# All high and low weights of a two-layer graph network moved to 32 modulo 128 bytes in each partition

## The chip, the cores and the metric

The kernel runs on one core of one Trainium2 chip. The metric is the device time in microseconds from start to end of one execution. A run of the kernel is an execution of one program; the median of three is compared.

## The reference

There are 50000 nodes with 256 features and 25000 edges with 64 features, sorted by target node. Everything is float32.

```python
h = relu(layernorm(x))                            # [50000, 256]
agg = segment_sum(edge_attr_64, dst, 50000)       # [50000, 64]
agg = agg / max(counts, 1)
hidden = relu(concat([agg, h], axis=1) @ W1 + b1) # W1 [320, 512]
out = x + hidden @ W2 + b2                        # W2 [512, 256]
```

## The kernel before

The nodes are cut into 98 tiles of 512 (`TILES`, `TILE`; the last has 336), and a tile into four groups of 128 (`SUB`). A tile goes through these stages, of which several tiles are under way at once, with X, HN, HQ, O and most other buffers in two copies:

- SyncE (SP) loads the node rows (`load_x`, L304) and for each group a window of edges (`load_windows`, L322 and L323), turns the normalised rows in quadrants (`move`), and stores the output (`store`).
- VectorE (DVE) takes the statistics and ScalarE (ACT) writes the normalised rows; DVE transposes them, and both split them into a high part that float32r holds exactly and a low rest (`HT_hi`, `HT_lo`). The means of the edge features come from a matmul with a one-hot matrix (`edge_means`, L893 to L898, reading `E_both` and `OH`) and lie in `QA` and `QB`.
- Layer 1 (`layer1_nodes`, L909 to L911, and `layer1_means`, L918 and L919) fills four PSUM banks, one for each 128 hidden units: high times high, high times low and low times high. In the matmuls of this layer the weights are the stationary operand, loaded by a weight load (PEld in the profile), and the activations are the moving operand of 512 columns.
- ACT writes the high half of the hidden layer (`H1_hi`, L611), DVE the low half (`H1_lo`, L729).
- Layer 2 (`layer2`) has the operands the other way round: the hidden layer is stationary, the weights `w2_both` move. L932 streams the high and the low weights of 128 hidden units in one go, 512 columns, against `H1_hi`; L934 streams the high ones alone, 256 columns, against `H1_lo`. DVE adds the halves and the residual (L740, L743).

The steps of layers 1 and 2 stand in `step`, whose order on TensorE (PE) is written out by hand: two groups of layer 1, the edge means of the next tile, two groups of layer 1, layer 2. Semaphores tie the engines together; each engine runs its own program in order.

The weights are read from memory once, in the start-up, into `w1_raw`, `wa_raw`, `ab_raw` and `w2_raw`. ACT copies them into the high tensors (`w1_hi`, `wa_hi`, `ab_hi`, and `w2_both[:, :, 0, :]` at L633), and GpSimd (POOL) subtracts these to get the low ones (`w1_lo`, `wb_lo`, and `w2_both[:, :, 1, :]` at L543). From then on TensorE alone reads them.

Every tensor in on-chip memory (SBUF) is a declaration `sb(name, shape)`, with the number of partitions first. The tensors lie one behind the other in each partition in the order of the declarations, each at the next multiple of 32 bytes. `ident`, the first, starts at a multiple of 128. The declarations up to the weights are these:

```python
        ident = sb("ident", [P, P])
        iota_row = sb("iota_row", [P, P])
        part_id = sb("part_id", [P, 1])
        base = sb("base", [P, TILES, SUB])
        half = sb("half", [P, SUB])
        eps = sb("eps", [P, SUB])
        ones_bf = sb("ones_bf", [P, 1], BF16)
        ones_f = sb("ones_f", [P, 1])
        b2_row = sb("b2_row", [P, D])
        w1_raw = sb("w1_raw", [P, CD, H])
        wa_raw = sb("wa_raw", [P, H])
        ab_raw = sb("ab_raw", [P, H])
        w2_raw = sb("w2_raw", [P, CH, D])
```

Here P is 128, D 256, H 512, CD 2, CH 4.

Of the kernel before, what the change touches and what calls it, by code (L numbers as in the profile page):

```python
# [14 lines left out]
P = 128  # L15
# [11 lines left out]
def build(nc, x, src, dst, edge_attr, w1, b1, w2, b2, out):  # L27
# [41 lines left out]
    with ExitStack() as ctx:  # L69
        def sb(name, shape, dt=F32):  # L70
            return ctx.enter_context(nc.sbuf_tensor(name, shape, dt))
# [18 lines left out]
        wa_raw = sb("wa_raw", [P, H])  # L90
        ab_raw = sb("ab_raw", [P, H])
        w2_raw = sb("w2_raw", [P, CH, D])
        w1_hi = sb("w1_hi", [P, CD, H], F32R)
        w1_lo = sb("w1_lo", [P, CD, H], F32R)
        wa_hi = sb("wa_hi", [P, H], F32R)
        wb_lo = sb("wb_lo", [P, H], F32R)
        ab_hi = sb("ab_hi", [P, H], F32R)
        w2_both = sb("w2_both", [P, CH, 2, D], F32R)


        dst_w = sb("dst_w", [EP, WIDE], I32)
# [920 lines left out]
```

## Time and profile before

| | us |
|---|---|
| median of 3 runs | 1345.34 (1344.73 to 1345.53) |
| the profiled execution, its own time | 1346.03 |
| its span, first to last instruction | 1344.4 |
| granted clock of TensorE over the span | 0.998 |

The profiled execution is one more run, 0.7 us above the median. Its span is 1.6 us less than its time, which is what lies around the instructions. In the page of the profile, busy time is a union of instruction durations per engine; a TensorE matmul's duration contains the tail of its pipeline, so that two neighbours overlap, and the distance between starts is what one costs. PE stands for the matmuls, PEld for the weight loads, which run beside the matmul ahead of them.

### The profile page before, as it was taken

What the parts mean: (1) busy time and instruction counts of PE and PEld (TensorE: products, weight loads), DVE (VectorE), ACT (ScalarE), POOL (GpSimd) and SP (SyncE); (2) the same over time, 40 slices, a digit from 0 to 9 for tenths busy, and PEclk for the clock granted to TensorE, in tenths of its full rate; (3) what the DMA queues carried; (4) which work ended last, traced back from release to release, by engine and by line L of the source; (5) the groups of instructions that cost most, each with busy time, mean ns of one, the idle gap of its engine ahead of it and who ended that gap; (6) DMA issues with size and microseconds to landing.
All of it is one profiled execution on the core that took longest, in us unless ns stands there. A gap on an engine that the chain in (4) does not pass through costs nothing.

```text
span 1344.4 us, 29244 instructions
## 1 busy us (share of the span) xinstructions
PE 1326.3 (99%) x6976; PEld 1118.6 (83%) x6976; DVE 1216.8 (91%) x3153; ACT 696.2 (52%) x1285; POOL 541.7 (40%) x707
## 2 busy tenths in 40 slices
PE   6999999999999999999999999999999999999998
PEld 3788888888888888888888888888888888888887
DVE  6899999999999999999999999999999999999997
ACT  5455555555555555555555555555555555555553
POOL 6443434343434343434343434343434343434341
PEclk9999999999999999999999999999999999999999
DMA  4676767676767676767676767676767666767663
GB/s 118 123 121 133 121 133 121 134 120 133 121 133 121 133 121 134 120 133 121 133 121 133 121 134 120 134 120 134 121 134 120 135 120 134 120 134 120 134 110 77
DMA packets 420692, 168.19 MB, mean 125 GB/s; under 512 B 319092, under 2 KB 420230, under 8 KB 420680
## 3 DMA queue, kind: packets, MB, share of 16 engines
q1 hardware_dynamic: 419688, 166.89, 66.8%
q10 hardware_dynamic: 992, 1.18, 0.3%
q14 instruction: 9, 0.07, 0.0%
q8 instruction: 3, 0.05, 0.0%
HBM read 66.25 MB, written 51.40 MB: 88 GB/s over the span
## 4 chain that ended last, share of the span: by engine, by line
PE 94%; SPq 2%; DVE 1%; DMA 1%; issue 1%; POOL 0%; ACT 0%; DVEq 0%; POOLq 0%
PE P L932 26%; PE P L934 13%; PE P L909 13%; PE P L911 13%; PE P L910 13%; PE P L918 6%; PE P L919 6%; PE PA L898 1%; PE PA L897 1%; DMA X<-in_x_dram 1%; SPq L322 0%; SPq L323 0%; SPq L310 0%; PE PA L893 0%; DMA dst_w<-in_dst_dram 0%
## 5 line engine op out<-in xcount | busy, mean ns | idle before, releaser
L932 PE MATMUL P<-w_both,H_hi 128*128 128x512 f32 x1564 | 558.8, 398 | 2.2 <-DVE H_lo L729 2.1
L611 ACT ACTIVATE H_hi<-P 128x512 fp32r<-128x512 f32 x392 | 233.1, 596 | 496.8 <-PE P L919 496.8
L934 PE MATMUL P<-w_both,H_lo 128*128 128x256 f32 x1564 | 440.3, 282 | 0.0
L932 PEld LDWEIGHTS P<-w_both,H_hi 128*128 128x128 f32 x1564 | 294.4, 188 | 75.5 <-DVE H_lo L729 3.2
L729 DVE SCALAR_TENSOR_TENSOR H_lo<-P,H_hi 128x512 fp32r<-128x512 f32 x392 | 266.4, 680 | 76.2 <-ACT H_hi L611 73.1
L909 PE MATMUL P<-HT_hi,w_hi 128*128 128x512 f32 x776 | 308.3, 397 | 0.0
L911 PE MATMUL P<-HT_hi,w_lo 128*128 128x512 f32 x776 | 304.3, 392 | 0.0
L910 PE MATMUL P<-HT_lo,w_hi 128*128 128x512 f32 x776 | 302.1, 389 | 0.0
L460 POOL TENSOR_TENSOR XB<-X,b_row 128x1024 f32<-128x1024 f32 x97 | 233.5, 2407 | 168.4 <-DVE O L743 165.9
L934 PEld LDWEIGHTS P<-w_both,H_lo 128*128 128x128 f32 x1564 | 294.2, 188 | 3.8
L454 POOL TENSOR_TENSOR E_both<-ES,E_both 128x256 fp32r<-128x256 f32 x98 | 72.9, 744 | 390.7 <-ACT E_both L591 390.7
L711 DVE STREAM_TRANSPOSE HT<-HQ 128x512 f32<-128x512 f32 x192 | 206.5, 1076 | 1.2 <-DMA HQ<-HN 1.1
L585 ACT ACTIVATE HN<-X,shift,rstd 128x256 f32<-128x256 f32 x388 | 200.3, 587 | 2.3 <-POOL shift L442 2.3
L597 ACT ACTIVATE HT_hi<-HT 128x512 fp32r<-128x512 f32 x192 | 121.5, 633 | 122.1 <-DVE HT L711 122.0
L743 DVE TENSOR_TENSOR O<-P,XB 128x256 f32<-128x256 f32 x391 | 166.0, 425 | 13.3
L911 PEld LDWEIGHTS P<-HT_hi,w_lo 128*128 128x128 f32 x776 | 145.6, 188 | 32.0
L909 PEld LDWEIGHTS P<-HT_hi,w_hi 128*128 128x128 f32 x776 | 145.8, 188 | 27.2
L740 DVE TENSOR_TENSOR XB<-P,XB 128x256 f32<-128x256 f32 x391 | 163.5, 418 | 4.5 <-PE P L934 1.5
L910 PEld LDWEIGHTS P<-HT_lo,w_hi 128*128 128x128 f32 x776 | 146.1, 188 | 24.6
L918 PE MATMUL P<-QA,wa_hi 128*128 128x512 f32 x392 | 153.1, 391 | 0.0
L919 PE MATMUL P<-QB,wb_lo 128*128 128x512 f32 x392 | 152.8, 390 | 0.0
L719 DVE TENSOR_TENSOR HT_lo<-HT,HT_hi 128x512 fp32r<-128x512 f32 x192 | 138.4, 721 | 10.3 <-ACT HT_hi L597 0.5
(85 smaller groups left out, 1190.7 us busy)
## 6 DMA issues: line engine op xcount, KB each, us to landing
out_dram<-O SPq DMA_DIRECT2D x97, 512.0 KB, 4.6
HQ<-HN SPq DMA_DIRECT2D x384, 128.0 KB, 4.1
X<-in_x_dram SPq DMA_DIRECT2D x95, 512.0 KB, 4.3
ER<-in_edge_attr_dram SPq DMA_DIRECT2D x392, 32.0 KB, 1.8
DT<-table_dram SPq DMA_DIRECT2D x392, 1.0 KB, 1.7
X<-in_x_dram ACTq DMA_DIRECT2D x1, 512.0 KB, 5.0
w_raw<-in_L_gnn_W_dram ACTq DMA_DIRECT2D x4, 128.0 KB, 5.0
w_raw<-in_L_gnn_W_dram SPq DMA_DIRECT2D x2, 256.0 KB, 4.5
```

The costliest lines, as they stand in the source:

```text
L460: pool.tensor_tensor(XB[b][:], rows_of(t, b), b2_row[:].unsqueeze(1).to_broadcast([P, SUB, D]), ALU.add).then_inc(s_xb, 1)
L585: act.activation(into, rows, ACT.Relu, bias=shift[b][:, j:j + 1], scale=rstd[b][:, j:j + 1]).then_inc(s_ln, 1)
L611: act.activation(H1_hi[:, m, nodes(t)], bank(m)[:, nodes(t)], ACT.Relu).then_inc(s_1hi, 1)
L711: dve.transpose(HT[:, c, :].rearrange("p (j n k) -> p k j n", j=SUB, k=QN), HQ[b][:, :, c * QP:(c + 1) * QP].rearrange("p (k j) f -> p k j ...
L729: dve.scalar_tensor_tensor(out=H1_lo[:, m, nodes(t)], in0=bank(m)[:, nodes(t)], scalar=0.0, in1=H1_hi[:, m, nodes(t)], op0=ALU.max, op1=AL ...
L909: pe.matmul(bank(m)[:, nodes(t)], w1_hi[:, c, cols], HT_hi[b][:, c, nodes(t)], start=(c == 0), stop=False)
L910: pe.matmul(bank(m)[:, nodes(t)], w1_hi[:, c, cols], HT_lo[b][:, c, nodes(t)], start=False, stop=False)
L911: pe.matmul(bank(m)[:, nodes(t)], w1_lo[:, c, cols], HT_hi[b][:, c, nodes(t)], start=False, stop=False)
L918: pe.matmul(bank(m)[:, nodes(t)], wa_hi[:, cols], QA[:, nodes(t)], start=False, stop=False)
L919: pe.matmul(bank(m)[:, nodes(t)], wb_lo[:, cols], QB[:, nodes(t)], start=False, stop=True).then_inc(s_l1, 1)
L932: pe.matmul(out_bank(j)[some, :], H1_hi[:, m, rows], w2_both[:, m, :, :].rearrange("p a d -> p (a d)"), start=(m == 0), stop=False)
L934: last = pe.matmul(out_bank(j)[some, 0:D], H1_lo[:, m, rows], w2_both[:, m, 0, :], start=False, stop=(m == CH - 1))
```

## The change

Two tensors that nothing reads or writes are declared, one of 24 float32 (96 bytes in each partition) ahead of the six weight tensors and one of 8 (32 bytes) behind them. Every instruction stays as it is, apart from the addresses in it.

```diff
@@ -90,12 +90,14 @@
         wa_raw = sb("wa_raw", [P, H])
         ab_raw = sb("ab_raw", [P, H])
         w2_raw = sb("w2_raw", [P, CH, D])
+        beside_w = sb("beside_w", [P, 24])
         w1_hi = sb("w1_hi", [P, CD, H], F32R)
         w1_lo = sb("w1_lo", [P, CD, H], F32R)
         wa_hi = sb("wa_hi", [P, H], F32R)
         wb_lo = sb("wb_lo", [P, H], F32R)
         ab_hi = sb("ab_hi", [P, H], F32R)
         w2_both = sb("w2_both", [P, CH, 2, D], F32R)
+        beside_x = sb("beside_x", [P, 8])
```

The line numbers of the profile are those of the kernel before.

## Rows read from the trace of the kernel before

**Rows 1.** The page: busy time of each engine, and the chain by engine.

```profile
PE 1326.3 (99%) x6976; PEld 1118.6 (83%) x6976; DVE 1216.8 (91%) x3153; ACT 696.2 (52%) x1285; POOL 541.7 (40%) x707
...
PE 94%; SPq 2%; DVE 1%; DMA 1%; issue 1%; POOL 0%; ACT 0%; DVEq 0%; POOLq 0%
```

**Rows 2.** Who TensorE waited for: us in total, times, longest.

```profile
PE P L959 <- ACT HN L585: 5.2, 1, 5.2
PE P L932 <- DVE H_lo L729: 2.1, 2, 1.7
```

**Rows 3.** One tile's stretch: length, busy us (instructions), clock, DMA share, GB/s.

```profile
699.50:712.94 13.44, 13.44 (x73) 11.39 (x72) 12.43 (x33) 7.04 (x14) 5.40 (x7) 1.00 0.68 127
```

**Rows 4.** By tile: ns min/median/max, first and last start in us, forms.

```profile
L909 PE MATMUL P<-HT_hi,w_hi x776: 312/394/442, 37.1 to 1336.2; 128*128 128x512 f32 x192, 128*128 128x336 f32 x2
...
L989 PE MATMUL P<-HT_lo,w_hi x8: 388/393/476, 25.8 to 27.5; 128*128 128x512 f32 x8
...
L633 ACT ACTIVATE w_both<-w_raw x1: 1058/1058/1058, 19.0 to 19.0; 128x1024 fp32r<-128x1024 f32 x1
L543 POOL TENSOR_TENSOR w_both<-w_raw,w_both x1: 2380/2380/2380, 24.3 to 24.3; 128x1024 fp32r<-128x1024 f32 x1
```

**Rows 5.** Timeline of TensorE, layer 1: start us, us, engine, line, operation.

```profile
704.09 0.39 PE L911 MATMUL P<-HT_hi,w_lo 128*128 128x512 f32 x1
...
704.77 0.39 PE L911 MATMUL P<-HT_hi,w_lo 128*128 128x512 f32 x1
705.01 0.39 PE L918 MATMUL P<-QA,wa_hi 128*128 128x512 f32 x1
705.23 0.39 PE L919 MATMUL P<-QB,wb_lo 128*128 128x512 f32 x1
705.46 0.39 PE L909 MATMUL P<-HT_hi,w_hi 128*128 128x512 f32 x1
...
706.84 0.39 PE L918 MATMUL P<-QA,wa_hi 128*128 128x512 f32 x1
707.07 0.39 PE L919 MATMUL P<-QB,wb_lo 128*128 128x512 f32 x1
707.29 0.39 PE L932 MATMUL P<-w_both,H_hi 128*128 128x512 f32 x1
```

**Rows 6.** Timeline of TensorE, layer 2 of the same tile.

```profile
708.00 0.40 PE L932 MATMUL P<-w_both,H_hi 128*128 128x512 f32 x1
708.23 0.28 PE L934 MATMUL P<-w_both,H_lo 128*128 128x256 f32 x1
708.35 0.40 PE L932 MATMUL P<-w_both,H_hi 128*128 128x512 f32 x1
...
712.59 0.40 PE L932 MATMUL P<-w_both,H_hi 128*128 128x512 f32 x1
712.82 0.28 PE L934 MATMUL P<-w_both,H_lo 128*128 128x256 f32 x1
712.94 0.39 PE L909 MATMUL P<-HT_hi,w_hi 128*128 128x512 f32 x1
```

**Rows 7.** Groups by line: count, busy us, mean ns, idle before.

```profile
L932 PE MATMUL P<-w_both,H_hi 128*128 128x512 f32 x1564 | 558.8, 398 | 2.2 <-DVE H_lo L729 2.1
L934 PE MATMUL P<-w_both,H_lo 128*128 128x256 f32 x1564 | 440.3, 282 | 0.0
...
L911 PE MATMUL P<-HT_hi,w_lo 128*128 128x512 f32 x776 | 304.3, 392 | 0.0
L910 PE MATMUL P<-HT_lo,w_hi 128*128 128x512 f32 x776 | 302.1, 389 | 0.0
...
L918 PE MATMUL P<-QA,wa_hi 128*128 128x512 f32 x392 | 153.1, 391 | 0.0
...
L910 PEld LDWEIGHTS P<-HT_lo,w_hi 128*128 128x128 f32 x776 | 146.1, 188 | 24.6
```

**Rows 8.** Timeline of the weight loads, beside the matmul start at 707.07.

```profile
707.07 0.19 PEld L932 LDWEIGHTS P<-w_both,H_hi 128*128 128x128 f32 x1
```

## The prediction

> **What bounds the kernel now.** I read the page first: its busy line has TensorE (PE) at 1326.3 of 1344.4 us, the vector engine (DVE) at 1216.8, the scalar engine (ACT) at 696.2, GpSimd (POOL) at 541.7, and the chain that ended last is TensorE for 94% of the span [rows 1]. The reader should look there for a single engine that is both always busy and the chain. A busy TensorE alone proves little, since its matmuls overlap, so the second view is the list of its waits: it waited 2.1 us in two places for the low half of the hidden layer, and everything else it waited for is in the start-up [rows 2]. The third view is the table by stretch. In one tile of 512 nodes out of the middle, 13.44 us long, TensorE is busy for all of it, DVE for 12.43, ACT for 7.04, POOL for 5.40, at a granted clock of 1.00 (the upper of the two levels, 2.4 GHz) [rows 3]. So the time is a sum of intervals between matmul starts and nothing else: about 37 us until layer 1 first runs in its steady form [rows 4], then a tile every 13.45 us, then a short end. Whatever lengthens or shortens one interval goes one to one into the result, up to the DVE's spare 1.0 us per tile.
>
> The fourth view is the timeline of TensorE, where I read starts, not durations (the durations hold a pipeline tail). In layer 1, from the start at 704.09 to that at 706.84 there are 12 matmuls of 128x512, so 2.75 / 12 = 0.229 us each; single intervals, rounded to 0.01, run from 0.22 to 0.24 [rows 5]. In layer 2 the matmuls come in pairs, 512 columns (L932) and 256 columns (L934); from 708.00 to 712.59 there are 13 pairs, 4.59 / 13 = 0.353 us, of which the 256 columns take 0.12 (0.118 as I take it) and the 512 the other 0.235 [rows 6]. The same shape thus takes 6 ns more in layer 2 than in layer 1. At 2.4 GHz, a column a cycle, 512 columns are 213 ns and 256 are 107, so layer 1 loses 16 ns per matmul and a layer-2 pair 33 ns. Something beyond columns costs time in every interval. Whether that something looks at the byte at which an operand starts is the whole question here.
>
> **The change, part by part.** The declarations are summed in order, each size rounded up to 32 bytes as the neighbouring small tensors are. From `ident` (which starts on a multiple of 128) to `w1_hi` lie 512 + 512 + 32 + 1568 + 4 x 32 + 1024 + 4096 + 2048 + 2048 + 4096 = 16064 bytes, which is 64 modulo 128. All of the six weight tensors have sizes that are multiples of 128, so all stand at 64 now, and a gap of 96 puts them at 32. The gap of 32 behind them completes 128, so everything declared later moves by a whole 128 bytes and keeps its place modulo 128. By the same sum the activations that meet the weights (`HT_hi`, `HT_lo`, `QA`, `QB`, `H1_hi`, `H1_lo`) stand at 0 modulo 128, before and after.
>
> Added instructions: none. Removed: none. No wait is added, and no queue (SP, ACT, POOL) gets another order. The gaps are never written. The transfers from memory go into the raw copies, which lie ahead of the first gap and don't move. What writes the moved tensors is a handful of operations in the start-up, such as the 1.06 us copy and the 2.38 us subtraction of `w2_both` [rows 4]; even a tenth more on these is under 0.4 us, and they lie beside other start-up work. I cost this at nothing, at most +0.4.
>
> What is left are TensorE's reads. Layer 1: 776 each of L909, L910, L911, 392 of L918 and as many of its twin L919, and three lines of 8 in the start-up (L970, L974, L989; one of them stands there) [rows 4, 7], 3136 in all. There the moved tensor is the stationary operand, read by the weight load. Such a load starts with the matmul ahead of it and takes 188 ns [rows 7, 8], inside an interval of 229; 41 ns of cover. Layer 2: 1564 L932 and 1564 L934 [rows 7]. There the moved tensor is the moving operand itself, streamed, and the loads read the hidden layer, which keeps its place; the pair of loads has 2 x 188 = 376 ns against a pair of 353, so no cover of that kind.
>
> No row of this trace has an operand of TensorE at 32 modulo 64: all start on multiples of 64. So the cost of the new place is bounded by the nearest rows. Toward zero: starts at 0 and at 64 modulo 128 can be compared for the load. Behind the last matmul of a layer-1 group (L919), the next load is at 0 (`H1_hi`) or at 64 (`w1_hi`), and the interval is 0.22 and 0.23 [rows 5]; behind L934 it is 0.12 with a load at 0 and 0.12 with one at 64 [rows 6]. A shift of 64 bytes in the stationary operand thus shows at most 0.01 us, the rounding. That is the nearest row to the edit, it is the same kind of edit at twice the size, and I take its value: 0 per matmul. Away from zero, in either direction: the only difference that one shape shows is the 6 ns between layers, whose operands stand differently (moving operand at 64 in layer 2, at 0 in layer 1), though the company of a short matmul differs too. As a gain it is 1564 x 6 ns = 9.4 us; as a loss it is 9.4 us if L932 alone pays again, 18.8 us if L934 does too.
>
> The Trainium skill, "TensorE: Matmul & The Clock Gate", section "Back-to-back issue gap", gives an isolated gap of N/2.4 + 2.5 ns, 216 ns for 512 columns, where the trace has 229 and 235; its Part 2 ("What happens when you issue a matmul") says that the weight load has a read port of its own and takes nothing from the running matmul. By these two together the placement could neither win nor lose. The excess that the trace has over that figure, 13 ns and 19 ns, contradicts at least one of them, and leaves open that the two reads do meet, which is what both rivals below live on.
>
> Sum for my forecast: the profiled run took 1346.0 us with a span of 1344.4; the edit adds 0, so a span of 1344.4 and, against the median of the runs shown, 1345.3.
>
> **Rivals.** *Faster, the layer-2 stream finds a better phase.* If two streams meet in the same memory, the relation of their starting bytes sets how often. Layer 2's 512-column interval is the longest of its shape (0.235 against 0.229), and its streams stand 64 bytes apart with the moving one at 64; moved to 32, it may fall to layer 1's value. For: the 6 ns are real, steady over all 13 pairs [rows 6], and TensorE waits for nobody. Against: layer 1's streams are 64 apart as well, and the 256-column neighbour may be the cause of the 6 ns. Price: 1564 x 6 ns = 9.4 us, giving 1335.9; with a few ns of layer 1 too, down to 1328. DVE would stay short of the bound (12.43 in a tile of 13.35).
>
> *Slower, a start off a 64-byte boundary costs one more piece.* Every TensorE operand now starts on a multiple of 64. If the memory is read in pieces of that size, 512 columns from 32 modulo 64 touch 33 pieces where they touched 32, and 256 columns 17 for 16. The place is layer 2, where the weights stream; it decides as soon as an extra piece is not swallowed by the start of the next matmul. Price: with the 6 ns that I have for a step, 9.4 us for L932 alone (1354.7), 18.8 for both (1364.1). In layer 1 the 41 ns of cover should take it. For: starts off 64 are new, and all intervals are strikingly regular, as if quantised. Against: nothing shows such a piece.
>
> *The change doesn't do what it says,* since the allocator may place tensors otherwise. The time is then that of the forecast too, and it can't be told from it by the time; it would take the addresses.
>
> **How the numbers follow.** No effect, 0.38: median 1345.3, own range 1344 to 1347. Faster, 0.30: 1336, reaching from 1328 to 1342. Slower, 0.32: 1355, reaching from 1349 to 1364. The likeliest is 1345.3. The range of 8 in 10 must take in most of both rivals: 1334 leaves out about a quarter of the faster case (0.08), 1358 about a third of the slower (0.11). What a measurement of this kernel can tell from no change is about 0.2%, 2.7 us; each rival's middle lies beyond it, so faster 0.30, same 0.38, slower 0.32.
>
> **What would show it.** In the timeline of a middle tile: 12 layer-1 intervals still 2.75 us, 13 pairs still 4.59, and the tile 13.45 by the starts of L893. If a pair falls to 0.347 with layer 1 unchanged, the faster rival is right; if it rises to 0.359 or 0.365, the slower. If layer-1 intervals move, the cover of 41 ns was no cover, and the stationary operand's start counts; the forecast then fails at the step where a shift of 64 stood for one of 32. New waits of TensorE for DVE would mean that its spare 1.0 us was less than I took it for.

## The result, and the profile after

The changed kernel takes 1348.24 us (median of 19 runs, 1347.18 to 1351.04) against 1345.57 for the kernel before (19 runs beside them, 1344.73 to 1347.97): a ratio of 1.0019, interval 1.0013 to 1.0026. It is 2.7 us slower. That lies inside the range I gave (1334 to 1358), but I had forecast no effect, and there is one: small only because two larger ones of opposite sign nearly cancel.

The profiled execution of the changed kernel was the longest of its runs, 1351.04 us with a span of 1349.4. The busy line, then the stretch of one middle tile (columns as in [rows 3]):

```profile
PE 1328.3 (98%) x6976; PEld 1115.3 (83%) x6976; DVE 1216.8 (90%) x3153; ACT 697.5 (52%) x1285; POOL 541.5 (40%) x707
```

```profile
703.26:716.73 13.47, 13.47 (x73) 11.36 (x72) 12.43 (x33) 7.07 (x14) 5.39 (x7) 1.00 0.68 127
```

TensorE is still busy for the whole tile, with the same instructions at the same clock; the tile is 0.03 us longer than in [rows 3]. To be exact about that, take the first edge-mean matmul of all tiles between 100 and 1300 us, once in the kernel before and once in the one after (ns min/median/max, then first and last start):

```profile
L893 PE MATMUL PA<-OH,E_both x89: 220/220/220, 111.5 to 1294.8; 128*128 128x128 f32 x89
```

```profile
L895 PE MATMUL PA<-OH,E_both x90: 222/223/223, 100.7 to 1299.8; 128*128 128x128 f32 x90
```

(1294.8 - 111.5) / 88 = 13.447 us a tile before, (1299.8 - 100.7) / 89 = 13.473 after: 0.026 more, times 97 tiles 2.6 us, which is the difference of the medians. (The other 2.4 us by which this one execution's span is longer lie in the start-up: its layer 1 first runs at 39.4 us, for 37.1 in [rows 4]. The medians, 2.7 us apart, don't show them.) Now the two layers, in the timeline of TensorE. Layer 1 first, the same 12 matmuls as in [rows 5]:

```profile
707.92 0.39 PE L913 MATMUL P<-HT_hi,w_lo 128*128 128x512 f32 x1
...
710.72 0.39 PE L920 MATMUL P<-QA,wa_hi 128*128 128x512 f32 x1
```

2.80 us where it was 2.75: 0.233 per matmul for 0.229. And 13 pairs of layer 2, as in [rows 6]:

```profile
711.88 0.39 PE L934 MATMUL P<-w_both,H_hi 128*128 128x512 f32 x1
712.11 0.28 PE L936 MATMUL P<-w_both,H_lo 128*128 128x256 f32 x1
712.23 0.39 PE L934 MATMUL P<-w_both,H_hi 128*128 128x512 f32 x1
...
716.39 0.39 PE L934 MATMUL P<-w_both,H_hi 128*128 128x512 f32 x1
```

4.51 us where it was 4.59: 0.347 per pair for 0.353. So the layer-2 rival came true with its 6 ns, and layer 1 gave all of it back and more. The unrounded starts say where each tile's 26 ns come from: 32 matmuls of layer 1 are 125 ns longer together (about 4 ns each), 16 pairs of layer 2 are 98 ns shorter (about 6 ns each).

### The profile page after: what moved, and what is told of

It reads as the page before. It is cut to its first block, busy times and chain, and to the rows that moved or that the text cites. A ratio compares the mean times of both kernels' runs of the same rounds, so it can differ in the third digit from the quotient of the medians.

```text
span 1349.4 us, 29244 instructions
## 1 busy us (share of the span) xinstructions
PE 1328.3 (98%) x6976; PEld 1115.3 (83%) x6976; DVE 1216.8 (90%) x3153; ACT 697.5 (52%) x1285; POOL 541.5 (40%) x707
## 4 chain that ended last, share of the span: by engine, by line
PE 93%; SPq 2%; DMA 2%; DVE 1%; issue 1%; POOL 0%; ACT 0%; DVEq 0%; POOLq 0%
PE P L934 25%; PE P L911 13%; PE P L936 13%; PE P L912 13%; PE P L913 13%; PE P L920 6%; PE P L921 6%; PE PA L900 1%; PE PA L899 1%; DMA HQ<-HN 1%; SPq L324 0%; SPq L325 0%; SPq L312 0%; SPq L285 0%; DMA dst_w<-in_dst_dram 0%
## 5 line engine op out<-in xcount | busy, mean ns | idle before, releaser
L934 PE MATMUL P<-w_both,H_hi 128*128 128x512 f32 x1564 | 548.0, 392 | 2.5 <-DVE H_lo L731 2.4
L912 PE MATMUL P<-HT_lo,w_hi 128*128 128x512 f32 x776 | 305.9, 394 | 0.0
```

What stands on the lines that cost most here:

```text
L912: pe.matmul(bank(m)[:, nodes(t)], w1_hi[:, c, cols], HT_lo[b][:, c, nodes(t)], start=False, stop=False)
L934: pe.matmul(out_bank(j)[some, :], H1_hi[:, m, rows], w2_both[:, m, :, :].rearrange("p a d -> p (a d)"), start=(m == 0), stop=False)
```

## The experiments

Below, *distance* means the start of the stationary operand's tensor less that of the moving one's, in bytes of the partition, modulo 256. All tensors of a layer agree in it, since their sizes and slices are multiples of 256. Before, layer 1 has distance 192 (weights at 64, activations at 128 modulo 256) and layer 2 has 64 (hidden layer at 128, weights at 64). The changed kernel has 160 (160 and 0) and 96 (0 and 160). The starts are summed from the declarations with `ident` at 128 modulo 256; were it at 0, all of them would be 128 further on, and the distances the same. All edits but those of the last two kernels only insert unused tensors; `[P, 8]` is 32 bytes. "Layer 1" is the 12 intervals read above, "pairs" 13 pairs; both from the timeline of TensorE between 700 and 725 us, the tile from starts as above, without their rounding where a third decimal matters.

**Each layer alone.** The two kernels undo one half of the change each. The first leaves the layer-2 weights at 64 modulo 128, the second those of layer 1.

```diff
+        gap0 = sb("gap0", [P, 24])
         w1_hi = sb("w1_hi", [P, CD, H], F32R)
...
+        gap1 = sb("gap1", [P, 8])
         w2_both = sb("w2_both", [P, CH, 2, D], F32R)
```

> The layer-1 weights alone start at 32 modulo 128 (96 bytes ahead of w1_hi, 32 ahead of w2_both, which stays at 64). Theory A, each layer pays for its own start: layer-1 triples take 0.700 us as in the changed kernel (0.687 before), layer-2 pairs 0.353 as before, tile about 13.58 us, time about 1345.5 + 13 = 1358.5. Theory B, the two layers are coupled through the order of matmuls, and only both moves together lengthen layer 1: triples 0.687, time 1345.5.

Measured: 1358.3 us (ratio 1.0094, 1.0077 to 1.0111); layer 1 2.80 us, pairs 4.60, tile 13.580. Those are the numbers of theory A; its reason did not survive the next run.

```diff
+        gap0 = sb("gap0", [P, 24])
         w2_both = sb("w2_both", [P, CH, 2, D], F32R)
...
+        gap1 = sb("gap1", [P, 8])
         dst_w = sb("dst_w", [EP, WIDE], I32)
```

> The layer-2 weights alone start at 32 modulo 128; the layer-1 weights stay at 64. Theory A: pairs take 0.347 us as in the changed kernel, layer-1 triples 0.687 as before, tile 13.34 us, time 1345.5 - 10.4 = 1335 (faster than both kernels). Theory B: no gain without the other move, pairs 0.353, time 1345.5.

Measured: 1351.04 us (ratio 1.004, 1.0025 to 1.0054). Neither theory foretold a slower kernel. The pairs did what A said, 4.52 us for 13; but layer 1, whose weights had not moved, was slow all the same:

```profile
706.42 0.39 PE L913 MATMUL P<-HT_hi,w_lo 128*128 128x512 f32 x1
...
709.23 0.39 PE L920 MATMUL P<-QA,wa_hi 128*128 128x512 f32 x1
```

2.81 us for 12. Something else than the start of the layer-1 weights had changed for layer 1.

**Other starts of the layer-2 weights.** The gaps around `w2_both` are 64 and 64, and 32 and 96.

```diff
+        gap0 = sb("gap0", [P, 16])
         w2_both = sb("w2_both", [P, CH, 2, D], F32R)
...
+        gap1 = sb("gap1", [P, 16])
         dst_w = sb("dst_w", [EP, WIDE], I32)
```

> The layer-2 weights start at 0 modulo 128, all else as before. If what counts is the start modulo 64 bytes (or its distance from the stationary operand's modulo 64), it is the same as before: pairs 0.353, time 1345.5. If the start modulo 128 counts, 0 stands as close to the hidden layer's 0 as it can, and the pair differs from 0.353 by at least 3 ns, the time by 5 us or more.

```diff
+        gap0 = sb("gap0", [P, 8])
         w2_both = sb("w2_both", [P, CH, 2, D], F32R)
...
+        gap1 = sb("gap1", [P, 24])
         dst_w = sb("dst_w", [EP, WIDE], I32)
```

> The layer-2 weights start at 96 modulo 128, all else as before. Modulo 64 alone: as with 32, pairs 0.347, time 1335. Modulo 128: another value than 0.347, the time differs from that of the kernel with 32 by 5 us or more.

Measured: 1353.84 us (ratio 1.0059, 1.0042 to 1.0076) with pairs 4.57, and 1354.18 (1.0061, 1.0045 to 1.0078) with pairs 4.55; layer 1 2.80 in both. The pair of e3 is 2 ns below that of before, less than the 3 ns I had asked for; the time of e4 is 3 us above e2, less than the 5. But neither pair has the value that the start modulo 64 foretold, so more than that counts. Layer 1 is slow in these too. What they share with the two before and with the changed kernel is the second gap: everything declared behind the weights went 128 bytes up, and I had called that no move.

**The later tensors alone, by 128 bytes.**

```diff
+        gap0 = sb("gap0", [P, 32])
         dst_w = sb("dst_w", [EP, WIDE], I32)
```

> Nothing moves but what is declared behind the weights: everything from dst_w on goes 128 bytes up, as it also did in the changed kernel and in the four before this one. Theory C, starts count modulo 128 or less: tile 13.447 us, layer-1 triples 0.687, pairs 0.353, time 1345.5. Theory D, the move of the activations by 128 bytes counts too (their starts modulo 256 change), and is what lengthened layer 1 where only the layer-2 weights had been moved: layer 1 near 0.233 per matmul, tile about 13.57 us, time about 1357.

Measured: 1352.72 us (ratio 1.0049, 1.0032 to 1.0065), tile 13.520. Theory D: with all weights where they were, layer 1 takes 2.81 us for 12 matmuls.

```profile
707.67 0.40 PE L912 MATMUL P<-HT_hi,w_lo 128*128 128x512 f32 x1
...
710.48 0.40 PE L919 MATMUL P<-QA,wa_hi 128*128 128x512 f32 x1
```

The time falls short of the 1357 I expected, since the pairs got shorter too (4.54), which I had not foreseen; in layer 2 the hidden layer had moved against the weights.

**The weights moved, the later tensors kept modulo 256.** The second gap is 128 bytes larger than in e2, in the changed kernel and in e1.

```diff
+        gap0 = sb("gap0", [P, 24])
         w2_both = sb("w2_both", [P, CH, 2, D], F32R)
...
+        gap1 = sb("gap1", [P, 40])
         dst_w = sb("dst_w", [EP, WIDE], I32)
```

> The layer-2 weights start at 32 modulo 128 as before in the run that moved them alone, but what is declared later goes 256 bytes up and keeps its start modulo 256. Theory C: as in that run, layer 1 at 0.233 per matmul, pairs 0.347, time 1351. Theory D: layer 1 back at 0.229, pairs 0.347, tile about 13.34, time about 1335.

Measured: 1338.72 us (ratio 0.9951, 0.9934 to 0.9968), tile 13.373. Layer 1 is back at 2.75 and the pairs are at 4.52; this is theory D, 3.7 us above the 1335 of it.

```diff
+        gap0 = sb("gap0", [P, 24])
         w1_hi = sb("w1_hi", [P, CD, H], F32R)
...
+        gap1 = sb("gap1", [P, 40])
         dst_w = sb("dst_w", [EP, WIDE], I32)
```

> The changed kernel with 128 more bytes in the gap behind the weights: weights at 32, what is declared later keeps its start modulo 256. Theory C: as the changed kernel, tile 13.473, time 1348.2. Theory D: another tile time, by 13 us in the sum if layer 1 goes back to 0.229 (about 1335).

Measured: 1350.13 us (ratio 1.0035, 1.0022 to 1.0047), tile 13.500, pairs 4.52. Another tile time, as D says, but layer 1 is not back: 2.80. Its distance is now 32.

```diff
+        gap0 = sb("gap0", [P, 24])
         w1_hi = sb("w1_hi", [P, CD, H], F32R)
...
+        gap1 = sb("gap1", [P, 40])
         w2_both = sb("w2_both", [P, CH, 2, D], F32R)
```

> The layer-1 weights alone start at 32; w2_both and all that is declared later go 256 bytes up and keep their starts modulo 256. Theory C: as in the run with only the layer-1 weights moved, triples 0.700, tile 13.580, time 1358.3. Theory D: triples back at 0.687 or at least other than 0.700, time below 1350.

Measured: 1355.59 us (ratio 1.0075, 1.0059 to 1.0092), tile 13.560. I expected below 1350, and missed: layer 1 takes 2.80 here too (distance 32 again), pairs 4.58. Put side by side by distance, the runs fall in line: layer 1 was fast at 192 and slow at 64, 160 and 32, and pairs with equal distance had equal times (64 in e1, e10 and before; 96 in e2 and after; 224 in e8 and e9). Of these only e1 against the other two at 64 has both operands at other starts modulo 256. That is theory E.

**Does the distance count, or a start?** Two kernels that move much and keep every distance: 256 bytes ahead of `dst_w`, and 32 bytes ahead of `w1_hi` with nothing behind.

```diff
+        gap0 = sb("gap0", [P, 64])
         dst_w = sb("dst_w", [EP, WIDE], I32)
```

> Nothing moves but what is declared behind the weights, by 256 bytes. Theory E, what counts is the distance between the start of the stationary and of the moving operand modulo 256 (so far 192 in layer 1 gave 0.229 and 64, 160 and 32 gave 0.233; 64 in layer 2 gave pairs of 0.353): distances as before, triples 0.687, pairs 0.353, tile 13.447, time 1345.5. Rival, modulo 512 or more: layer 1 or the pairs change, the time differs by 3 us or more.

```diff
+        gap0 = sb("gap0", [P, 8])
         w1_hi = sb("w1_hi", [P, CD, H], F32R)
```

> One gap of 32 bytes ahead of w1_hi and none behind: the weights and everything declared later go 32 bytes up together, so all of TensorE's operands of the steady tiles start at 32 modulo 64, at the distances of before. Theory E: tile 13.447, time 1345.5 up to what transfers and other engines do with the new starts. Rival, a start off a 64-byte boundary costs a piece more in itself: layer 1 and the pairs longer by 3 ns or more each, time 1355 or more.

Measured: 1345.84 us (ratio 1.0000, 0.9990 to 1.0009) and 1347.46 (1.0015, 1.0005 to 1.0025). In both the tile is that of before:

```profile
L894 PE MATMUL PA<-OH,E_both x89: 220/220/220, 111.9 to 1295.2; 128*128 128x128 f32 x89
```

```profile
L894 PE MATMUL PA<-OH,E_both x89: 220/220/221, 111.7 to 1295.1; 128*128 128x128 f32 x89
```

13.447 us in both by the unrounded starts; the mean of each of the 71 intervals of a tile agrees with before within 0.1 ns. In the second one every operand of layers 1 and 2 starts at 32 modulo 64: a start off 64 costs TensorE nothing. Its 1.7 us in the median are not in the regular tile. Its profiled execution had a span of 1345.8, 1.3 above before; 1.1 of that is one interval of TensorE near the end, which waits for DVE (`H1_lo`) until 1316.32. What made DVE late is not shown.

**Filling the list of distances.** In e13 both layers have 0, in e14 128 and 32.

```diff
+        gap0 = sb("gap0", [P, 16])
         w1_hi = sb("w1_hi", [P, CD, H], F32R)
...
+        gap1 = sb("gap1", [P, 48])
         dst_w = sb("dst_w", [EP, WIDE], I32)
```

> All operands of TensorE in the steady tiles start at 128 modulo 256: distance 0 in both layers (64 bytes ahead of w1_hi, 192 behind w2_both). Theory E foretells pairs of 0.350 from the run that had layer 2 at distance 128 only if distances repeat modulo 128; otherwise a new value. For layer 1 untried: between 0.226 and 0.237. A natural guess, that equal alignment is best, would give a tile under 13.3 us and a time under 1335.

```diff
+        gap0 = sb("gap0", [P, 48])
         w1_hi = sb("w1_hi", [P, CD, H], F32R)
...
+        gap1 = sb("gap1", [P, 24])
         w2_both = sb("w2_both", [P, CH, 2, D], F32R)
...
+        gap2 = sb("gap2", [P, 56])
         dst_w = sb("dst_w", [EP, WIDE], I32)
```

> Distance 128 in layer 1 and 32 in layer 2, both untried. Theory E: the two layers take values of their own, whatever the other has. If modulo 128 were enough, layer 1 would be as at 0 in the run with both at 0, and the pairs as at 160, 0.350.

Measured: 1343.3 us (ratio 0.9983, 0.9973 to 0.9992), tile 13.420, and 1357.07 (1.0083, 1.0066 to 1.0100), tile 13.570. Equal alignment everywhere is not the best: layer 1 gains (0.227 per matmul after five to seven slower ones at the start of each pair of groups), while the pairs are at their worst, 4.59 us for 13. A repeat modulo 128 is refuted: in both layers 64 and 192 give different times (before against e7).

```diff
+        gap0 = sb("gap0", [P, 40])
         w1_hi = sb("w1_hi", [P, CD, H], F32R)
...
+        gap1 = sb("gap1", [P, 48])
         w2_both = sb("w2_both", [P, CH, 2, D], F32R)
...
+        gap2 = sb("gap2", [P, 40])
         dst_w = sb("dst_w", [EP, WIDE], I32)
```

> Distance 96 in layer 1 (untried), 224 in layer 2. Theory E, each layer's interval follows from its own distance modulo 256: pairs 0.346 as in both runs with 224, whatever layer 1 does; layer 1 between 0.226 and 0.237. Rival, the pairs' value depends on how layer 1 hands over: pairs away from 0.346 by 2 ns or more.

```diff
+        gap0 = sb("gap0", [P, 8])
         w1_hi = sb("w1_hi", [P, CD, H], F32R)
...
+        gap1 = sb("gap1", [P, 48])
         w2_both = sb("w2_both", [P, CH, 2, D], F32R)
...
+        gap2 = sb("gap2", [P, 8])
         dst_w = sb("dst_w", [EP, WIDE], I32)
```

> Distance 224 in layer 1 (untried), 96 in layer 2. Theory E: pairs 0.347 as in both runs with 96; layer 1 has a value of its own, with which the list of the eight distances is complete for both layers. If 224, 32 bytes short of 0, were good as 0 and 192 are, the time would be about 1336.

Measured: 1350.74 us (ratio 1.0035, 1.0023 to 1.0048) and 1349.32 (1.0030, 1.0019 to 1.0042). Pairs 4.51 in both, as their distances say, and layer 1 slow in both, 2.80: 224 isn't good.

**The best of each layer together.**

```diff
+        gap0 = sb("gap0", [P, 16])
         w1_hi = sb("w1_hi", [P, CD, H], F32R)
...
+        gap1 = sb("gap1", [P, 8])
         w2_both = sb("w2_both", [P, CH, 2, D], F32R)
...
+        gap2 = sb("gap2", [P, 40])
         dst_w = sb("dst_w", [EP, WIDE], I32)
```

> The best distance so far in each layer: 0 in layer 1 (0.227 in the steady part of a group), 224 in layer 2 (pairs 0.346). Theory E: the tile of the run with both at 0, 13.420 us, less 16 x (0.354 - 0.346) = 0.12, so 13.30 to 13.34 us, and a time near 1334, faster than before and than any run so far. Rival, a group's start state decides more than the distance: layer 1 does not reach 0.227, the time stays above 1338.

Measured: 1335.45 us (ratio 0.9922, 0.9905 to 0.9938), faster than both kernels, by 10 us against before. The tiles, and the pairs of one of them:

```profile
L896 PE MATMUL PA<-OH,E_both x90: 220/220/220, 111.0 to 1297.7; 128*128 128x128 f32 x90
```

```profile
715.48 0.40 PE L935 MATMUL P<-w_both,H_hi 128*128 128x512 f32 x1
...
720.00 0.39 PE L935 MATMUL P<-w_both,H_hi 128*128 128x512 f32 x1
```

(1297.7 - 111.0) / 89 = 13.334 us a tile, 4.52 for 13 pairs. Theory E gave 13.30 to 13.34. The best kernel differs from the one before in three gaps alone, of 64, 32 and 160 bytes.

All of it in one table. Interval and pair are means of the unrounded starts over the cycle in which each layer settles, in ns; an entry that several kernels share is theirs within 0.1 ns.

| distance | layer 1, one matmul of 512 | kernels | layer 2, pair of 512 and 256 | kernels |
|---|---|---|---|---|
| 0 | 226.7 (after some slower ones) | e13, e17 | 353.3 | e13 |
| 32 | 233.3 | e9, e10 | 353.3 | e14 |
| 64 | 233.3 | e2, e3, e4, e7 | 353.3 | before, e1, e10, e11, e12 |
| 96 | 234.3 | e15 | 346.7 | after, e2, e16 |
| 128 | 232 to 233, irregular | e14 | 351.1 | e3 |
| 160 | 233.3 | after, e1 | 350.0 | e4 |
| 192 | 228.9 | before, e8, e11, e12 | 348.9 | e7 |
| 224 | 233.3 | e16 | 346.7 | e8, e9, e15, e17 |

Two limits of this table. Most rows stand for one place of the tensors: other starts at the same distance were run at 192 in layer 1 (e12) and at 64 (e1, e12) and 96 (e16) in layer 2, and there the values held. And the two values don't give the tile: the changed kernel, e2, e9 and e16 share 233.3 and 346.7, and their tiles are 13.473, 13.507, 13.500 and 13.487 us. Up to 34 ns a tile depend on how one stretch of matmuls follows another.

**Where the distance alone does not decide.** The last tile has 336 nodes, so its layer 1 streams 336 columns. There e3 and e2 part, although all their layer-1 operands start at the same places modulo 256 (distance 64); only layer 2, which has run before, differs. The start of the ninth of its 32 matmuls and that of the last, 23 intervals, first in e2, then in e3:

```profile
1338.28 0.32 PE L911 MATMUL P<-HT_hi,w_hi 128*128 128x336 f32 x1
...
1341.87 0.32 PE L921 MATMUL P<-QB,wb_lo 128*128 128x336 f32 x1
```

```profile
1341.97 0.32 PE L911 MATMUL P<-HT_hi,w_hi 128*128 128x336 f32 x1
...
1345.50 0.32 PE L921 MATMUL P<-QB,wb_lo 128*128 128x336 f32 x1
```

3.59 / 23 = 0.156 us against 3.53 / 23 = 0.153, each in a steady cycle; e4 and e7 are like e2, and every complete kernel whose layer 1 is at another distance takes 0.153 to 0.154. So theory E holds for the regular tile; in this one, what ran before also decides in which cycle a stretch settles, and most of what the distance costs at 512 columns is absent.

**Do the other engines get in the way?** Wherever a distance changes, the weights move against all that VectorE, ScalarE, GpSimd and the transfers touch, and not only against TensorE's other operand. The end of the run separates the two. In the kernel before, nothing but TensorE works from 1338.19 to 1339.67 (columns as in [rows 3], transfers at 0.00):

```profile
1338.19:1339.67 1.48, 1.48 (x10) 1.28 (x9) 0.00 (x1) 0.00 (x0) 0.00 (x0) 1.00 0.00 0
```

```profile
1338.41 0.40 PE L932 MATMUL P<-w_both,H_hi 128*128 128x512 f32 x1
...
1339.47 0.40 PE L932 MATMUL P<-w_both,H_hi 128*128 128x512 f32 x1
```

Three pairs take 1.06 us, 0.353 each, as in the middle of the run; in the changed kernel, with the others silent from 1343.24 to 1344.67, three pairs take 1.04, 0.347 each. In layer 2 the effect is TensorE's own. Layer 1 has no such quiet stretch.

**Is it the load that gets in the way?** In e17 an interval grows from 153.3 ns at 336 columns (last tile) to 226.7 at 512, which is 0.417 ns a column, one cycle at 2.4 GHz. So I count 213 ns of each 229 for the columns. If the weight load beside the stream caused the other 16, a load of half the columns should halve them. In both kernels half of the hidden units are left out: all matmuls of layer 1 are cut in the same way, in all tiles but the first; e19 has the gap of e7 as well.

```diff
-                cols = slice(m * P, (m + 1) * P)
+                cols = slice(m * P, m * P + 64)
...
-                    pe.matmul(bank(m)[:, nodes(t)], w1_hi[:, c, cols], HT_hi[b][:, c, nodes(t)], start=(c == 0), stop=False)
+                    pe.matmul(bank(m)[0:64, nodes(t)], w1_hi[:, c, cols], HT_hi[b][:, c, nodes(t)], start=(c == 0), stop=False)
```

> The kernel before, with layer 1 of the steady tiles loading 64 columns of stationary weights instead of 128 (half of the hidden units are left out, the loads last half as long; columns streamed, addresses and distances stay). Theory F, the excess over 213 ns (16 ns here) comes of the weight load reading while the matmul streams: it halves, intervals about 0.221, tile about 0.24 us shorter. Rival, the excess belongs to the start of every matmul, load or no load: intervals stay at 0.229.

> The same halved loads with everything behind the weights 128 bytes up (distance 64 instead of 192 in layer 1, which cost 4.4 ns per matmul with full loads). Theory F: the excess of 20 ns halves to 10, intervals about 0.223, so the distance costs about 2 ns instead of 4.4. Rival: 0.233 as with full loads.

Measured, one execution each: 1340.41 and 1345.04 us, beside 1344.79 of the kernel before. The loads take 134 ns instead of 188, so 29% less and not the half that I had expected; the matmul intervals hardly change (timeline of all engines in e18: a load, then 12 matmuls' first and last):

```profile
702.22 0.13 PEld L911 LDWEIGHTS P<-HT_hi,w_lo 128*64 128x64 f32 x1
```

```profile
701.76 0.39 PE L911 MATMUL P<-HT_hi,w_lo 128*64 128x512 f32 x1
...
704.50 0.39 PE L919 MATMUL P<-QA,wa_hi 128*64 128x512 f32 x1
```

2.74 us for 12, 0.228 each, where theory F asked for 0.221, or for 0.225 if the excess went by the time of the load (16 x 134 / 188 = 11); in e19 2.79, 0.233 each, where it asked for 0.223. The rival holds for layer 1, with one execution of each kernel and a steady cycle in both: most of the excess doesn't scale with the length of the load, and neither does what the distance costs (0.05 us over 12 matmuls in both sizes). Both tiles are 0.073 us shorter than with full loads; in e18, by the starts, 52 ns of that are the one interval behind the short edge means, about what the load beside it got shorter (54 ns). Layer 2 had no such run. The last tile's group of 80 nodes has short loads there (148 ns) and only three pairs of them: 345 ns each before, where the tile has 353, but 353 in e16, where it has 347. Something about that group, its load or its smaller output, thus counts in layer 2, and not in one direction; no run separates them.

## Why the prediction was wrong

**That TensorE's intervals set the time** held. The difference of the tiles times 97 gives the difference of the medians within 0.7 us in every complete kernel but e12: +0.026 x 97 = 2.6 us after (measured 2.7), -0.113 x 97 = -11.0 for e17 (measured -10.5). In e12 the tile says 0 and the median 1.7, of which the profiled execution shows one wait for DVE near the end; so a change of addresses can cost something outside the intervals.

**"Keeps its place modulo 128"** is the first step that failed. I costed the 128 bytes that the later tensors move at nothing, as a matter of words in the change, without any row that showed that a place modulo 128 was enough. That move alone costs 7.5 us (e7, 0.073 x 97 = 7.1 by the tile); the move of the weights on top of it gives 4.5 us back (1352.7 to 1348.2). Of the change as measured, then, the gap behind the weights is the loss, and the gap ahead of them, given that loss, a gain. In place of "no move" the runs showed that layer 1 leaves its distance of 192 modulo 256: 32 matmuls a tile at about 4 ns more. If the gap behind had held 160 bytes instead of 32, the change would have cost 5.0 us (e9) and not 2.7: layer 1 then stands at distance 32, where it is as slow as at 160, and of the 27 ns more per tile half lie, by the starts, in the first pairs of layer 2 and the rest at the other hand-overs.

**"A shift of 64 bytes shows at most 0.01 us, so 0 per matmul"** is the second. The runs showed 4 ns per matmul more in layer 1 and 6 per pair less in layer 2 in its place. The rows compared two loads behind the same kind of matmul, at one hand-over between groups each, to 0.01 us; the effect is 0.004 per matmul and shows only where the same hand-over repeats. A sum of 12 or 13 intervals resolves it, and I had such sums, but only for one place each. The row nearest in bytes was not the nearest in kind.

**The faster rival** had the mechanism half right: what counts is indeed the relation of two starts, and its size for the pairs, 6 ns, was met (0.353 to 0.347). Its reason against itself, that layer 1's streams are 64 apart as well, was wrong by the modulus: 64 one way and 64 the other are 192 and 64 modulo 256, and these are 228.9 and 233.3 ns in layer 1. And it let layer 1 stay as it was or gain a few ns, where layer 1 lost 125 ns a tile.

**The slower rival** gave the right sign for the wrong reason. A start off a 64-byte boundary costs nothing (e12), and its place, layer 2, became faster. Its other half, that 41 ns of cover would shield layer 1, failed too: layer 1 got slower with its loads still hidden, and with loads of 134 ns instead of 188 the distance cost the same (e18 against e19).

**The rule weighed.** I had weighed the rule of the Trainium skill, "TensorE: Matmul & The Clock Gate" ("What happens when you issue a matmul"), that a weight load reads through a port of its own and takes nothing from the running matmul. That halving the load leaves the interval agrees with it; that the interval depends on the distance between the two operands does not follow from it, nor from the fixed 2.5 ns of "Back-to-back issue gap". The Trainium skill gives that 2.5 ns for an isolated matmul. I had taken the trace's excess over it as speaking against one of the two statements, but the trace is a stream with loads, so the excess alone did not.

**What stays open.** Why the distance counts, and why with a period of 256 bytes, is not shown; neither is why some cycles depend on what ran before. Which stationary operand matters, the one being loaded for the next matmul or the one in use, can't be told here, since both have the same distance within a layer. That the other engines have no part in it is shown for layer 2 alone. I also can't say why a distance of 224, between the two good ones of 192 and 0, is bad for layer 1.

## What to carry to other kernels

Where one engine's instruction intervals are the whole time, compare sums over a dozen or more equal intervals, per layer, before and after: a median within 0.2% can hide two effects of 0.9% and 0.7% (125 and 98 ns of 13447). When a layout is changed, list the starts of every operand that meets the moved one, modulo 256 at least, since padding "back to the same place" is only as good as the modulus. It can pay to try the eight 32-byte distances between stationary and moving operands for each layer, in the whole kernel and not one layer at a time; of the 15 combinations run here the best is worth 10 us of 1345, and the worst costs 13. The values of the table are those of float32r, 512 columns and this order of matmuls; at 336 columns most of the differences were gone.

## What the runs showed of the hardware

- The time from one matmul to the next, same shape and clock (2.4 GHz granted), depends on the distance between the starts of its operands modulo 256 bytes: 226.7 to 234.3 ns for 512 columns, 346.7 to 353.3 ns for a pair of 512 and 256. Equal starts are best in one layer and worst, with distances of 32 and 64, in the other. For the pairs this holds with all other engines idle (0.353 before, 0.347 after).
- The distance is not all: at 336 columns and the same starts modulo 256, layer 1 settled at 0.156 us a matmul in e2 and at 0.153 in e3.
- Where both operands start together made no difference in the two moves tried: all 71 intervals of a tile agree within 0.1 ns when everything moves by 32 bytes together, or the activations alone by 256.
- Intervals repeat in short cycles (225.8, 229.2, 231.7 ns in layer 1 before; 235.0 and 118.3 in its layer 2), and a tile's length was a whole number of 6.667 ns, within 0.04 ns, in every kernel but one (13.447 us is 2017 of them, 13.473 is 2021, 13.373 is 2006, 13.333 is 2000). The one is e14, whose tiles take 13.560 and 13.580 us in turn, 2034 and 2037. That something with this period sets when a matmul can start is a guess from these lengths; no run shows what it is.
- Halving the columns of a hidden weight load shortened the load from 188 to 134 ns and left the interval of the matmul beside it in layer 1 (0.229 to 0.228 us).
